# Graph kernel on one Trainium2 core: the edge counts and the edge weights stored as two separate matrices, not interleaved by 100 columns

## Reference

```
x = _layernorm(x + _L0_gnn_ref(x, src, dst, edge_weight, L0_gnn_weight, L0_gnn_b))   # GCN: weighted sum over edges
x = _layernorm(x + _L1_gnn_ref(x, edge_index, ...))       # GAT: softmax over edges, 4 heads
x = _layernorm(x + _L2_gnn_ref(x, ...))                   # attention over edges
x = _layernorm(x + _L3_gnn_ref(x, ...))                   # SAGE: two mean aggregations
# GCN, the layer whose loads the text speaks of most:
xw = x @ weight
msgs = edge_val[:, None] * xw[edge_col]
out = relu(segment_sum(msgs, edge_row, num_segments=N_NODES) + b)
```

## Time and profile before

| | |
|---|---|
| time before, median of 3 runs | 2224.72 us (2222.59 to 2229.77) |
| the profiled execution's own time | 2222.41 us |
| its span in the profile | 2220.7 us |
| mean granted PE clock | 0.963 of full |
| DVE busy | 1751.0 us (79%) |
| PE busy | 1847.6 us (83%) |
| DMA packets of all kinds | 482577, of which 322696 under 512 B |

### The profile page before, as it was taken

The page is one execution under the profiler, slowest core; times in us unless marked ns, Lnnn a source line. Parts: engine busy times, 40 slices in busy tenths (PEclk is TensorE's granted clock), DMA queues, the critical chain, the costliest instruction groups (busy, mean ns, idle before and its releaser), DMA issues. The chain is left out here.

```text
span 2220.7 us, 43460 instructions
## 1 busy us (share of the span) xinstructions
PE 1847.6 (83%) x16094; PEld 1415.3 (64%) x16095; DVE 1751.0 (79%) x1831; ACT 1195.8 (54%) x2209; POOL 115.0 (5%) x225
## 2 busy tenths in 40 slices
PE   3666666799778888888888888894899999899997
PEld 2666665344467666676667666674688888755655
DVE  5999998000589999999999999976688888677276
ACT  1566665000586767767777677765666666500201
POOL 4000000100000000000000000000000000011010
PEclk9999999899999999999999999986899999999999
DMA  4789998999043144413442144324355555299193
GB/s 113 217 250 250 251 250 243 252 272 272 17 120 73 51 120 120 120 27 95 120 120 63 58 120 120 91 62 89 89 119 118 118 118 148 91 383 394 64 409 149
DMA packets 482577, 341.91 MB, mean 154 GB/s; under 512 B 322696, under 2 KB 474528, under 8 KB 475856
## 3 DMA queue, kind: packets, MB, share of 16 engines
q1 hardware_dynamic: 476864, 337.05, 54.7%
q10 hardware_dynamic: 4928, 2.20, 0.4%
q0 software_dynamic: 720, 1.77, 0.3%
HBM read 214.05 MB, written 126.94 MB: 154 GB/s over the span
## 5 line engine op out<-in xcount | busy, mean ns | idle before, releaser
L1082 ACT ACTIVATE exponentials<-gr_ps,att_cols 128x256 f32<-128x256 f32 (+1 forms) x1300 | 488.6, 486 | 184.2 <-PE gr_ps L937 181.9
L937 PE MATMUL gr_ps<-ident,gr_r 128*128 128x128 f32 (+1 forms) x2500 | 377.6, 291 | 70.7 <-DVE gr_r L1289 68.8
L937 PEld LDWEIGHTS gr_ps<-ident,gr_r 128*128 128x128 f32 (+1 forms) x2500 | 283.0, 148 | 152.2 <-issue 128.8
L970 PE MATMUL gr_ps<-exponentials,heads 128*33 128x128 f32 (+1 forms) x5000 | 357.6, 276 | 14.1 <-DVE exponentials L1295 14.1
L1295 DVE SCALAR_TENSOR_TENSOR exponentials<-exponentials,gr_count_t 128x3072 f32<-128x3072 f32 (+1 forms) x104 | 341.2, 3281 | 24.8 <-ACT exponentials L1082 24.2
L1256 DVE CUSTOM_DVE_ANT_0 gr_unread<-gr_src_rows,gr_closed 128x3125 bf16<-128x3125 f32 (+1 forms) x100 | 344.3, 3443 | 14.3 <-ACT gr_src_rows L1136 13.9
L571 PE MATMUL bm_ps<-bm_hot 128*100 128x100 bf16 (+1 forms) x3168 | 221.6, 225 | 106.9 <-DVE bm_hot L522 106.9
L970 PEld LDWEIGHTS gr_ps<-exponentials,heads 128*33 128x33 f32 x5000 | 250.4, 112 | 78.2 <-issue 51.4
L571 PEld LDWEIGHTS bm_ps<-bm_hot 128*100 128x100 bf16 x3168 | 205.1, 125 | 123.5 <-DVE bm_hot L522 123.5
L605 ACT ACTIVATE bm_stage<-bm_ps 96x800 f32<-96x800 f32 x264 | 206.3, 829 | 122.6 <-PE bm_ps L571 119.6
L522 DVE TENSOR_TENSOR bm_hot<-bm_hot,near 128x2400 bf16<-128x2400 bf16 x132 | 185.8, 1408 | 18.9
(11 more groups left out here) (308 smaller groups left out, 1996.2 us busy)
## 6 DMA issues: line engine op xcount, KB each, us to landing
adjacency<-bm_stage SPq DMA_DIRECT2D x264, 300.0 KB, 3.3
count_pair<-adjacency SPq DMA_DIRECT2D x37, 1600.0 KB, 8.6
count_more<-count_by_source SPq DMA_DIRECT2D x30, 1600.0 KB, 8.5
count_by_source<-gr_count_t SPq DMA_DIRECT2D x12, 3200.0 KB, 17.2
gr_src_rows<-adjacency SPq DMA_DIRECT2D x20, 1600.0 KB, 15.1
count_pair<-count_by_source SPq DMA_DIRECT2D x20, 1600.0 KB, 8.7
count_more<-adjacency SPq DMA_DIRECT2D x13, 1600.0 KB, 8.4
gr_count_t<-adjacency SPq DMA_DIRECT2D x5, 1600.0 KB, 14.9
```

The lines of the kernel that those rows point to most:

```text
L937: last = pe.transpose(ps[:, i % RINGS, c:c + n], r[0:n, slot(g, h) + j, s * P:(s + 1) * P], k.ident[0:n, 0:n])
L970: last = pe.matmul(ps[j * PAIR:j * PAIR + C + 1, 7, 0:rows(g)], heads[:, h, s, :], e[:, s, c:c + rows(g)], start=s == 0, stop=s == NT - 1, ...
L1082: last = act.activation(e[:, s, places(g, h)], ps[:, i % RINGS, c:c + w], ACT.Exp, bias=cols[:, h, s:s + 1])
```

## The change

`adjacency` becomes two matrices, counts and weights, one behind the other, each with contiguous rows of 3200 floats. SP stores each half of a lap with two DMAs instead of one, one for counts and one for weights, so each semaphore `stored[u][h]` rises by 32 where it rose by 16. The runs of a store are 100 floats, 400 bytes. The buffer `stage` in SBUF keeps its layout. A tile of a reader is now 128 runs of 3200 floats, 12.8 KB. All arithmetic is the same.

```
-            sp.dma_start(k.adj_rest, nought[:]).then_inc(cleared, 16)
+            sp.dma_start(k.adj_rest, nought[:].rearrange("p (v c) -> p v c", v=2)).then_inc(cleared, 16)
...
-                    act.wait_ge(stored[u][h], nth * 16 + 16)
+                    act.wait_ge(stored[u][h], nth * 32 + 32)
...
             def store(lap, u, nth):
                 for h in range(2):
                     sp.wait_ge(copied, lap * 2 + (5 + h))
-                    sp.dma_start(k.adj_w[:, bass.ds(lap * LW + HALF_LW * h, HALF_LW), :],
-                                 stage[:, u, HALF_LW * h:HALF_LW * (h + 1)].rearrange("p w v c -> p w (v c)")
-                                 ).then_inc(stored[u][h], 16)
+                    for v in range(2):
+                        sp.dma_start(k.adj_w[v][:, bass.ds(lap * LW + HALF_LW * h, HALF_LW), :],
+                                     stage[:, u, HALF_LW * h:HALF_LW * (h + 1), v]).then_inc(stored[u][h], 16)
...
-    return sp.dma_start(tile.rearrange("p (t h l) -> p t h l", t=1, l=SL), matrix[:, bass.ds(t, 1)])
+    return sp.dma_start(tile.unsqueeze(1), matrix[:, bass.ds(t, 1)])
...
-    adj = dram("adjacency", (2 * NP * NP,))
-    k.adj_w = adj[0:2 * ROWS * NP].rearrange("(w p c) -> p w c", p=KEYS, c=2 * SL)
-    k.adj_rest = adj[2 * ROWS * NP:2 * NP * NP].rearrange("(p c) -> p c", p=P)
-    by_part = adj.rearrange("(t p h v l) -> v p t h l", p=P, h=HI, v=2, l=SL)
-    k.count_rs = by_part[0]
-    k.weight_rs = by_part[1]
+    adj = dram("adjacency", (2, NP * NP))
+    k.adj_w = adj[:, 0:ROWS * NP].rearrange("v (w p c) -> v p w c", p=KEYS, c=SL)
+    k.adj_rest = adj[:, ROWS * NP:NP * NP].rearrange("v (p c) -> p v c", p=P)
+    by_row = adj.rearrange("v (t p c) -> v p t c", p=P, c=NP)
+    k.count_rs = by_row[0]
+    k.weight_rs = by_row[1]
```

More of the change, by code:

```diff
@@ L595, in _ @@
                 for h in range(2):
-                    act.sem_inc(stored[s][h], 16)
+                    act.sem_inc(stored[s][h], 32)
             act.sem_inc(redo_copied, 1)
-            act.sem_inc(redo_stored, 16)
+            act.sem_inc(redo_stored, 32)
             def copy_out(lap, u, nth):
@@ L609, in redo @@
                 act.wait_ge(redo_used, end + 1)
-                act.wait_ge(redo_stored, begin * 16 + 16)
+                act.wait_ge(redo_stored, begin * 32 + 32)
                 act.activation(stage[:, 0, 0].rearrange("p v c -> p (v c)"), ps[0:KEYS, 0, 0:WIDE], ACT.Copy
@@ L615, in redo @@
                 act.wait_ge(redo_copied, end + 1)
-                act.dma_start(k.adj_w[:, bass.ds(w, 1), :], stage[:, 0, 0:1].rearrange("p w v c -> p w (v c)")
-                              ).then_inc(redo_stored, 16)
-                act.wait_ge(redo_stored, begin * 16 + 32)
+                for v in range(2):
+                    act.dma_start(k.adj_w[v][:, bass.ds(w, 1), :], stage[:, 0, 0:1, v]).then_inc(redo_stored, 16)
+                act.wait_ge(redo_stored, begin * 32 + 64)
                 with act.Fori(begin + 1, end) as at:
-                    act.sem_inc(redo_stored, 16)
+                    act.sem_inc(redo_stored, 32)
             each_lap(act, copy_out)
@@ L624, in _ @@
                 for h in range(2):
-                    act.wait_ge(stored[s][h], 16 * (LAPS // 2) + 16)
+                    act.wait_ge(stored[s][h], 32 * (LAPS // 2) + 32)
             each_crowded(act, redo)
@@ L639, in _ @@
                 for h in range(2):
-                    sp.wait_ge(stored[s][h], 16 * (LAPS // 2) + 16)
+                    sp.wait_ge(stored[s][h], 32 * (LAPS // 2) + 32)
 def tile_columns(t, width=D, per_bank=4):
```

## The result

| | before | after |
|---|---|---|
| median | 2223.65 us (4 runs) | 2386.94 us (4 runs) |
| span of the profiled execution | 2220.7 us | 2384.7 us |

The ratio is 1.073, 95% interval 1.0713 to 1.0748: the change makes the kernel 7.3% slower. The forecast was 0.7% slower, and 2387 lies outside its range of 2203 to 2320.

The account below looks back on a forecast made before the run. DVE was taken to bound the build, with DMA close behind, and 400-byte reads the GCN sums. 2222.4 + 33 (build) - 16 (GCN) = 2239, or 2242 against the median; predicted 2240 us, range 2203 to 2320.

Parts of the forecast that it names:

- The place and the chain: Build: DMA engines become the bound at 2.71 us a lap; ACT waits for stores, PE for ACT's copies, DVE for PE.
- SP's four issues: Build: four issues of 0.32 us, 1.27 us of a 2.454 us lap, hidden by DVE's lap at no cost.
- the page's DMA share of 0.90: Build: DVE sets the lap of 2.454 us, but the DMA engines are close behind at share 0.90.
- 11 us for the period: GCN sums: tiles fall from 6.01 to PE's own 5.50 us apart, saving 0.51 us over about 21 periods.
- 5 for the start: GCN sums: the first tile's load lands earlier with 12.8-KB runs, saving 4.1 to 6.3 us, taken as 5.
- GAT and attention: GAT: earlier landings worth nothing, DVE being 98% busy; attention: at most one wait of 1.9 us, left in the range.
- what does a 400-byte write cost: Build: the step that decides the sign; 28.2 ns a packet taken, between bounds of 23.5 and 46.1 ns.
- a line times 1.22: Build: 23.5 ns from the line between 264 and 512 bytes, scaled as 800-byte packets exceed their line, gives 28.7 ns.
- my 33: Build: loss in us from a lap of 2.71 instead of 2.454 us over about 130 laps.
- my two signs of being wrong in the build: Build, new profile: DVE's lap still 2.45 us (packet under 25.6 ns), or over 4 us (price does not fall with bytes).
- The rival of a price per packet, 46.1 ns,: Build: a packet costs by number, not bytes; lap 4.43 us, + 257 us, time 2465; chance 0.13.

Follow-up runs that it names:

- experiment 2: Kernel before, interleaved 800-byte runs kept, but each half stored by two DMAs, four transfers a lap; 2226.98 us against 2224.16.
- experiment 1: Kernel before, interleaved layout and readers kept, but each half stored by two DMAs of 400-byte runs; 2272.49 us beside 2224.16.
- experiments 4 and 9: Changed kernel with each 400-byte run in a 512-byte slot, at the slot's start (2239.94 us) or with both matrices 256 bytes later (2243.87 us).
- experiments 9 to 12: Changed kernel with slots of 512 bytes at offsets 256 and 192 bytes (2243.87, 2323.85 us), then slots of 768 at 0 and 192 (2253.93, 2322.82 us).
- experiment 6: Changed kernel with each 400-byte run in a slot of 464 bytes, 64 bytes free between runs; 2304.49 us beside 2225.87 for the kernel before.
- experiment 8: Changed kernel with four stage buffers, a lap's four stores split by even and odd partitions; 2310.23 us, against 2329.14 when split by halves.

## Why the prediction missed

*The place and the chain were right.* The build is where the sign is decided; the stores become the bound, and the wait goes from ACT to PE to DVE. SP's four issues cost nothing (experiment 2). That the page's DMA share of 0.90 was the margin to look at was right as well.

*GCN was right, and a little small.* I had 11 us for the period and 5 for the start, 16. Measured are 20.4: the tiles came at 5.3 to 5.5 us, mostly 5.37, not 5.50, and the first 5.5 us earlier. GAT and attention gave nothing, as forecast; 2.8 us behind GCN are unexplained and small.

*The step that failed is "what does a 400-byte write cost".* I took 28.2 ns, from the nearest sustained write and from a line times 1.22. For a 400-byte run in the interleaved layout that is nearly right: experiment 1 has 29.2 ns by the lap, and 48 us against my 33. But I gave the runs one price wherever they lie, and the changed kernel pays 39.3 ns by its lap (3.77 us / 96). That lap lies between my two signs of being wrong in the build, 2.45 and over 4 us, so neither would have told. My 1.22 had folded the addresses into one factor taken from 800-byte runs. The experiments split the 1.32 us that a lap lost so:

- Runs of 400 instead of 800 bytes, at the best addresses: 2.58 - 2.454 = 0.13 us (experiments 4 and 9).
- Addresses off the 256-byte blocks: 2.80 - 2.58 = 0.22 us. In the dense layout a run begins on some multiple of 16 bytes, and half of these 16 positions make it span three blocks. Half of 3.17 - 2.58 is 0.30 us, so 2.88 is expected; the interleaved kernel, whose runs begin on the same 16 positions, measures 2.80. That is an estimate, since experiments 9 to 12 leave open which property of the address counts.
- The rest, 3.77 - 2.80 = 0.97 us, is the two matrices. Interleaved, the runs of one transfer have gaps of 400 bytes; in two matrices they touch. Gaps of 64 bytes take back 0.72 of it (experiment 6), and what goes with the gaps, or with writing neighbours in different transfers (experiment 8), is the packets over 200 ns. So runs of one transfer that touch are shown as the cause. How the chip comes by it is not shown. Slots of 448 and 464 bytes, with gaps of 48 and 64 bytes, are still 0.15 to 0.17 us above the 2.88 that their addresses give, and no experiment settled that.

*The rival of a price per packet, 46.1 ns,* would have given 2465. It was nearer in time than my forecast but is wrong as a mechanism: the same 1536 packets cost 0.13 us a lap in good places. The same holds for the rule quoted from the Trainium skill ("DMA: Bandwidth & Descriptors", Specifications) that runs under 512 B bring a read-modify-write: 400-byte writes ran at 237 GB/s in slots of 512 bytes, 26.9 ns a run by the lap, less than the 28.2 of a 512-byte one.

Another section of that page of the Trainium skill speaks to the addresses ("How a descriptor splits into AXI transactions"): for a descriptor that does not begin on a 256-byte boundary the first transaction starts at the boundary below, and the bytes before the start are fetched unused and still cost beats. For offset 192 that is an estimate of 6 more beats of 32 B, 7.1 ns a packet at the page's 850 MHz, and none for offset 256. The laps agree in direction and roughly in size: (3.17 - 2.58) / 96 = 6.1 ns for writes at offset 192, and nothing at 256. But the packets themselves rose by only 1.9 ns a run (0.18 us / 96), so this is no proof of that mechanism. The page speaks of fetching, and reads showed no difference: 272 GB/s in GCN at offset 0 and at 192. The section would have warned of the middle term; it says nothing of the largest.

*What I should have asked.* The diff moves the runs of one transfer next to each other and off any boundary. The prediction compared lengths of runs only, took its price from a row whose addresses are tidy (512 bytes), and let the range end at 34 ns.

PE's granted clock was 0.78 to 0.79 in the build, where it was 1.00 before. PE waits for ACT there, up to 3.4 us at a time, so I take the clock to follow from the stall. Standing still does not always bring it down: at offset 192, with a lap of 3.17 us and waits of at most 2.4 us, it was 0.95. Whether the clock adds to the lap was not tried.

## What to carry to other kernels

When a layout is changed to suit the readers, price the writer's packets by length, by the place of each run in its 256-byte block, and by whether one transfer writes runs that touch. Here the reader's 20 us cost the writer 181. A DMA share of 0.90 behind another engine's bound is little slack: an added microsecond of DMA becomes a stall of everything. A mean packet time can hide what matters: here the median stayed at 24 ns, and one packet in a hundred was over 200. And where a store is late at times, try deeper buffers: they took back a third of the lap's loss here, though not its cause.

## What was not expected of the hardware

The same 400-byte writes, the same number a lap, took 2.58, 2.67, 2.80, 3.03, 3.05, 3.17 or 3.77 us, by nothing but their addresses in DRAM. Reads did not care: 400-byte reads ran at 272 GB/s, interleaved at multiples of 400 bytes and in slots of 512 alike. And deeper buffers that took back 0.47 us of a lap in the dense layout took back 0.06 in slots of 512 with the padding, where the engines were full (share 1.00).
